# Thresholds of a sparsemax attention: stretched Newton steps, and flagged heads found by rank

## The reference, cut to what matters

```python
x = x + xattn(layernorm(x), ctx)      # q, k, v, o with biases; weights = sparsemax(q k^T / sqrt(32)) over 722 keys
x = x + ffn(layernorm(x))             # sqrt((x cos(theta + n1))^2 + (x sin(phi + n2))^2)

def sparsemax(x):                     # per row: the tau with sum(max(x - tau, 0)) = 1
    zs = -jnp.sort(-x, axis=-1)
    rho = jnp.arange(1, L + 1)
    cssv = jnp.cumsum(zs, axis=-1) - 1.0
    k = jnp.maximum(jnp.sum(zs > cssv / rho, axis=-1, keepdims=True), 1)
    tau = jnp.take_along_axis(cssv, k - 1, axis=-1) / k
    return jnp.clip(x - tau, 0.0)
```

## Time and profile before

| | us |
|---|---|
| median of 3 runs (846.85 to 848.14) | 847.61 |
| the profiled execution, its own time | 848.82 |
| its span | 847.0 |
| DVE busy | 653.7 (77%) |
| PE busy | 600.7 (71%) |
| ACT busy | 373.8 (44%) |
| POOL busy | 205.9 (24%) |
| mean granted clock of PE, share of full speed | 0.84 |

### The profile page before, as it was taken

One profiled execution on the slowest core, in us unless ns is written; L12 is line 12 of the kernel. 1 busy time (PEld: TensorE's weight loads), 2 busy tenths in 40 slices (PEclk: granted clock), 3 DMA queues, 4 the chain that ended last, 5 costly groups with the idle time before them and its releaser, 6 DMA issues.

```text
span 847.0 us, 14807 instructions
## 1 busy us (share of the span) xinstructions
PE 600.7 (71%) x4592; PEld 341.7 (40%) x4592; DVE 653.7 (77%) x3044; ACT 373.8 (44%) x653; POOL 205.9 (24%) x242
## 2 busy tenths in 40 slices
PE   4687228437986099989458998896386498897584
PEld 2344114224543065456233654563143354465251
DVE  5999659659697399999559888996696599999900
ACT  3444216217663056467225565663153265554231
POOL 3643402201403014032301332234004032121101
PEclk9678758858998589999768999999598699997857
DMA  9541110200032000312120212231201101020000
GB/s 324 184 130 44 49 49 3 58 7 25 19 91 57 18 25 17 94 30 70 40 69 0 70 31 56 71 82 28 80 2 55 24 22 48 21 60 11 1 11 10
DMA packets 33458, 44.16 MB, mean 52 GB/s; under 512 B 8347, under 2 KB 26779, under 8 KB 33376
## 3 DMA queue, kind: packets, MB, share of 16 engines
q1 hardware_dynamic: 32320, 41.09, 17.0%
q10 hardware_dynamic: 1056, 2.10, 0.7%
HBM read 23.77 MB, written 1.64 MB: 30 GB/s over the span
## 4 chain that ended last, share of the span: by engine, by line
PE 40%; DVE 30%; issue 18%; ACT 6%; DVEq 2%; DMA 1%; SPq 1%; POOL 1%; POOLq 0%
PE ring L452 19%; DVE cand L913 9%; PE ring L518 6%; PE ring L594 3%; PE mix_bank L567 3%; PE ring L542 3%; PE ring L491 2%; DVE dif L928 2%; DVE f_sum L938 2%; PE ring L503 2%; DVE over L932 2%; ACT S L669 1%; ACT qst L669 1%; DVE dif L933 1%; DVE n_over L940 1%
## 5 line engine op out<-in xcount | busy, mean ns | idle before, releaser
L913 DVE MAX8 cand<-S 100x8 f32<-100x45 f32 (+1 forms) x2048 | 223.1, 189 | 12.3 <-issue 5.2
L452 PE MATMUL ring<-wv,ctx 128*121 128x512 f16 x576 | 161.7, 401 | 0.0
L452 PE MATMUL ring<-ctx,wk 128*128 128x361 f16 x768 | 134.9, 337 | 4.5 <-DVE ctx L1069 4.5
L582 PE MATMUL ring<-ident,tt 100*3 100x100 f16 x128 | 10.7, 244 | 157.3 <-issue 153.0
L785 ACT ACTIVATE pT<-ring 121x800 f32<-121x800 f32 x96 | 80.5, 839 | 85.5 <-PE ring L594 85.5
L669 ACT ACTIVATE S<-ring 100x722 f32<-100x722 f32 x128 | 95.4, 774 | 30.4 <-PE ring L542 29.7
L328 POOL TENSOR_TENSOR ctx<-ctx_f,ctx 128x484 f16<-128x484 f32 x42 | 51.6, 1228 | 211.8 <-ACT ctx L669 211.3
L452 PEld LDWEIGHTS ring<-ctx,wk 128*128 128x128 f16 x768 | 78.4, 104 | 57.7 <-issue 14.1
L669 ACT ACTIVATE qst<-ring 96x800 f16<-96x800 f32 (+1 forms) x32 | 25.7, 829 | 171.8 <-PE ring L582 161.7
L542 PE MATMUL ring<-kst,qst 96*100 96x361 f16 x256 | 68.7, 360 | 29.6 <-ACT S L669 12.5
L452 PEld LDWEIGHTS ring<-wv,ctx 128*121 128x121 f16 x576 | 73.8, 141 | 35.1 <-issue 9.9
(11 more groups left out here) (127 smaller groups left out, 817.2 us busy)
## 6 DMA issues: line engine op xcount, KB each, us to landing
kst<-ks SPq DMA_DIRECT2D x384, 45.1 KB, 1.9
ctx_f<-in_ctx SPq DMA_DIRECT2D x45, 242.0 KB, 2.9
xq<-in_x SPq DMA_DIRECT2D x8, 200.0 KB
xr<-in_x SPq DMA_DIRECT2D x8, 200.0 KB
out_y<-att SPq DMA_DIRECT2D x8, 200.0 KB
S<-in_L_xattn_Wk ACTq DMA_DIRECT2D x1, 1024.0 KB, 6.9
wq<-in_L_xattn_Wq ACTq DMA_DIRECT2D x1, 1024.0 KB, 11.5
wcos<-in_L_ffn_theta SPq DMA_DIRECT2D x1, 1024.0 KB, 10.4
```

The costliest lines, as they stand in the source:

```text
L452: last = nc.tensor.matmul(psum, lhs(c, i), w(c, j), start=(c == 0 and n == 0), stop=(c == DC - 1 and n == 2))
L913: last = nc.vector.max(cand[:, h, 8 * n:8 * n + 8], S[0:L, HH * (i % 2) + h, cuts[n]:cuts[n + 1]])
```

## The change

The stretch factors multiply the first two Newton steps (1.15 and 1.1). The last round looks at seven ranks instead of eight; the first estimate comes from the top value of each piece alone. The eighth rank enters the flag as a count of pieces whose eighth value is below tau, added to the same sum, so `n_edge`, its reduction and its matmul are gone. In `settle`, flagged heads get their number plus one as a code, MAX8 sorts the codes downward, and the sorted list is cast to integers. Its first word says whether there is anything to do; if so, that head is refined directly, then the second word is read, and only if it is not zero a loop of seven turns runs over the rest of the list. `refine` makes one Newton step instead of two ahead of its test, and the test is reduced to one word on DVE (five small maxima) and read with one load instead of four. `NEWTON_MAX` stays 28.

```diff
@@ -26,7 +26,8 @@
 LN_EPS = 1e-5
 SUM_TOL = 1e-5
 PIECES = 16
-RANKS = (2, 4, 6, 8)
+RANKS = (2, 4, 6, 7)
+STRETCH = (1.15, 1.1, 1.0, 1.0)
 NEWTON_MAX = 28
 TINY = 2.0 ** -20
 SCRATCH = 2048
@@ -149,12 +150,13 @@
         dif, over = sb("dif", [L, HH, NCAND]), sb("over", [L, HH, NCAND], BF16)
         fold = sb("fold", [L, HH, 2 + NCAND // 2], BF16)
         tau = sb("tau", [L, 2, HH])
-        f_sum, step_t, n_over, n_now, n_edge = (sb(n, [L, HH]) for n in ("f_sum", "step_t", "n_over", "n_now", "n_edge"))
+        f_sum, step_t, n_over, n_now = (sb(n, [L, HH]) for n in ("f_sum", "step_t", "n_over", "n_now"))
         zero, minus = sb("zero", [L, 1]), sb("minus", [L, 1])
-        flag_i, any_i = sb("flag_i", [1, HH], I32), sb("any_i", [1, 1], I32)
+        order_c, code, ranked = (sb(n, [1, HH]) for n in ("order_c", "code", "ranked"))
+        ranked_i = sb("ranked_i", [1, HH], I32)
         again, againT = sb("again", [P, 32]), sb("againT", [P, 32])
-        again_m = sb("again_m", [P, 1])
-        again_i = sb("again_i", [P, 1], I32)
+        again_m = sb("again_m", [1, P // 32])
+        again_i = sb("again_i", [1, 1], I32)
         count, inv_count, new_sum, delta = (sb(n, [L, 1]) for n in ("count", "inv_count", "new_sum", "delta"))
         eps_t = sb("eps_t", [L, 1])
         st1, mv1, sd1 = sb("st1", [L, 6]), sb("mv1", [L, 2]), sb("sd1", [L, 2])
@@ -526,8 +528,7 @@
                 if i > 0:
                     pe.wait_ge(aT_ready, 2 * i)
                 nc.tensor.matmul(flag_ps, ones[:, :], n_over[:, :], start=True, stop=False)
-                nc.tensor.matmul(flag_ps, minus[:, :], n_now[:, :], start=False, stop=False)
-                nc.tensor.matmul(flag_ps, ones[:, :], n_edge[:, :], start=False, stop=True).then_inc(flag_sum, 1)
+                nc.tensor.matmul(flag_ps, minus[:, :], n_now[:, :], start=False, stop=True).then_inc(flag_sum, 1)
 
             def scores(i, heads):
                 b, part = divmod(i, 2)
@@ -919,9 +920,9 @@
                 t4 = t.rearrange("p (g a c) -> p g a c", a=1, c=1)
                 pieces = cand[:, :, :].rearrange("p g (n r) -> p g n r", r=8)
                 after(found)
-                n = counted(nc.vector.tensor_reduce(f_sum[:, :], pieces[:, :, :, 0:2], AXY, ALU.add))
+                n = counted(nc.vector.tensor_reduce(f_sum[:, :], pieces[:, :, :, 0], AX, ALU.add))
                 after(n)
-                n = counted(nc.vector.tensor_scalar(t, f_sum[:, :], -1.0, 1.0 / (2 * PIECES), ALU.add, ALU.mult))
+                n = counted(nc.vector.tensor_scalar(t, f_sum[:, :], -1.0, 1.0 / PIECES, ALU.add, ALU.mult))
                 for turn, ranks in enumerate(RANKS):
                     E = PIECES * ranks
                     after(n)
@@ -944,23 +945,24 @@
                     n = counted(nc.vector.scalar_tensor_tensor(step_t[:, :], f_sum[:, :], -1.0, step_t[:, :],
                                                                ALU.add, ALU.mult))
                     after(n)
-                    last = nc.vector.tensor_tensor(t, t, step_t[:, :], ALU.add)
+                    last = nc.vector.scalar_tensor_tensor(t, step_t[:, :], STRETCH[turn], t, ALU.mult, ALU.add)
                     if turn < len(RANKS) - 1:
                         n = counted(last)
                 last.then_inc(tau_ready, 1)
                 dve.wait_ge(tau_ready, i + 1)
-                n = counted(nc.vector.tensor_tensor(
-                    over[:, :, :].rearrange("p g (n r) -> p g n r", r=8), pieces,
-                    t4.broadcast_to([L, HH, PIECES, 8]), ALU.is_ge))
+                marks = over[:, :, :].rearrange("p g (n r) -> p g n r", r=8)
+                counted(nc.vector.tensor_tensor(marks[:, :, :, 7:8], pieces[:, :, :, 7:8],
+                                                t4.broadcast_to([L, HH, PIECES, 1]), ALU.is_lt))
+                n = counted(nc.vector.tensor_tensor(marks[:, :, :, 0:7], pieces[:, :, :, 0:7],
+                                                    t4.broadcast_to([L, HH, PIECES, 7]), ALU.is_ge))
                 after(n)
-                n_edge_at = counted(nc.vector.tensor_reduce(
-                    n_edge[:, :], over[:, :, :].rearrange("p g (n r) -> p g n r", r=8)[:, :, :, 7], AX, ALU.add))
                 n = counted(nc.vector.tensor_tensor(fold[:, :, 2:2 + NCAND // 2], over[:, :, 0:NCAND // 2],
                                                     over[:, :, NCAND // 2:NCAND], ALU.add))
                 after(n)
                 n = counted(nc.vector.reduce_sum(n_now[:, :], fold[:, :, :], AX))
                 after(n)
-                nc.vector.tensor_tensor(n_now[:, :], n_now[:, :], n_over[:, :], ALU.min).then_inc(flag_ready, 1)
+                nc.vector.scalar_tensor_tensor(n_now[:, :], n_now[:, :], -float(PIECES), n_over[:, :],
+                                               ALU.add, ALU.min).then_inc(flag_ready, 1)
 
             def newton(p, t, n, total):
                 nc.vector.tensor_scalar(mask_row, p, 0.0, None, ALU.is_gt, ALU.add,
@@ -979,26 +981,28 @@
                 dve.wait_ge(fix, n + 6)
                 return n + 6
 
-            def refine(i, h):
-
-                t = tau[:, i % 2, bass.ds(h, 1)]
-                row = S[0:L, bass.ds(h + HH * (i % 2), 1), :].rearrange("p a n -> p (a n)")
+            def refine(i, number):
+
+                number = nc.s_assert_within(number, 1, HH, skip_runtime_bounds_check_because="inside If(number > 0)")
+                t = tau[:, i % 2, bass.ds(number - 1, 1)]
+                row = S[0:L, bass.ds(number - 1 + HH * (i % 2), 1), :].rearrange("p a n -> p (a n)")
                 dve.sem_clear(fix)
                 nc.vector.scalar_tensor_tensor(relu_row, row, t, zero[:, :].broadcast_to([L, N]),
                                                ALU.subtract, ALU.max, accum_out=new_sum[:, :]).then_inc(fix, 1)
                 dve.wait_ge(fix, 1)
                 n = newton(relu_row, t, 1, new_sum[:, :])
-                n = newton(relu_row, t, n, new_sum[:, :])
                 nc.vector.tensor_scalar(again[0:L, 0:1], new_sum[:, :], 1.0 + SUM_TOL, None, ALU.is_gt).then_inc(fix, 1)
                 dve.wait_ge(fix, n + 1)
                 nc.vector.transpose(againT[:, :], again[:, :]).then_inc(fix, 1)
                 dve.wait_ge(fix, n + 2)
-                nc.vector.reduce_max(again_m[:, :], againT[:, :], AX).then_inc(fix, 1)
-                dve.wait_ge(fix, n + 3)
-                nc.vector.tensor_copy(again_i[:, :], again_m[:, :]).then_inc(fix, 1)
-                dve.wait_ge(fix, n + 4)
-                left = [dve.value_load(again_i[32 * q:32 * q + 1, 0:1], min_val=0, max_val=1) for q in range(P // 32)]
-                with dve.If(left[0] + left[1] + left[2] + left[3] > 0):
+                for q in range(P // 32):
+                    nc.vector.reduce_max(again_m[0:1, q:q + 1], againT[32 * q:32 * q + 1, :], AX).then_inc(fix, 1)
+                n += 2 + P // 32
+                dve.wait_ge(fix, n)
+                nc.vector.reduce_max(again_i[:, :], again_m[:, :], AX).then_inc(fix, 1)
+                dve.wait_ge(fix, n + 1)
+                left = dve.value_load(again_i[0:1, 0:1], min_val=0, max_val=1)
+                with dve.If(left > 0):
                     with dve.Fori(0, NEWTON_MAX) as _:
                         dve.sem_clear(fix)
                         newton(relu_row, t, 0, new_sum[:, :])
@@ -1018,18 +1022,26 @@
                 dve.wait_ge(fix, 5)
 
             def settle(i):
+
                 dve.sem_clear(check_step)
                 dve.wait_ge(flag_sum, i + 1)
-                nc.vector.tensor_copy(flag_i[:, :], flag_ps).then_inc(check_step, 1)
-                nc.vector.reduce_max(any_i[:, :], flag_ps, AX).then_inc(check_step, 1)
+                nc.vector.scalar_tensor_tensor(code[:, :], flag_ps, 0.5, order_c[:, :],
+                                               ALU.is_gt, ALU.mult).then_inc(check_step, 1)
+                dve.wait_ge(check_step, 1)
+                nc.vector.max(ranked[:, :], code[:, :]).then_inc(check_step, 1)
                 dve.wait_ge(check_step, 2)
-                todo = dve.value_load(any_i[0:1, 0:1], min_val=0, max_val=2 * L * NCAND)
-                with dve.If(todo > 0):
+                nc.vector.tensor_copy(ranked_i[:, :], ranked[:, :]).then_inc(check_step, 1)
+                dve.wait_ge(check_step, 3)
+                first = dve.value_load(ranked_i[0:1, 0:1], min_val=0, max_val=HH)
+                with dve.If(first > 0):
                     dve.wait_ge(tau_split, i + 1)
-                    with dve.Fori(0, HH) as h:
-                        rows = dve.value_load(flag_i[0:1, bass.ds(h, 1)], min_val=0, max_val=2 * L * NCAND)
-                        with dve.If(rows > 0):
-                            refine(i, h)
+                    refine(i, first)
+                    second = dve.value_load(ranked_i[0:1, 1:2], min_val=0, max_val=HH)
+                    with dve.If(second > 0):
+                        with dve.Fori(1, HH) as k:
```

(5 more changed lines are left out.)

## The result

The changed kernel takes 821.59 us (four runs, 821.17 to 823.80); the kernel before, on the same chip, 847.23 us. The ratio is 0.9709, 95% interval 0.9679 to 0.9738. The forecast was 816 us, range 802 to 833.

What follows compares the result with a forecast made beforehand. PE and DVE take turns, with PE idle while DVE sits in flagged settles. Terms -92.7 - 12.5 + 78.3 - 5 = -31.9 on 848.8 us give 816.9; the median lies 1.2 lower, so 816 us, range 802 to 833.

Steps and rivals of the forecast that it cites:

- The heads and the loop: Flagged heads fall from seven to three, in settles 3 and 10; head 3 of settle 3 enters the 28-step loop.
- Four settles to the plain path: Four of six flagged settles lose their flags, each falling to 1.13 us: -92.7 us, taken in full.
- The loop: In settle 3, 28 Newton turns of 3.15 us each, 88.2 us, hidden by nothing.
- The rest of the settle: Settle 3 without its 28-step loop: lead-in, two refinements, loads, six idle turns at 1.36 us and the split, 24.6 us.
- Settle 3 as a whole: Settle 3 keeps both flagged heads and gains the 28-step loop: 24.6 + 88.2 - 34.5 = +78.3 us.
- Settle 10: Settle 10 keeps one flagged head, refined without the loop: 9.9 us against 22.4, so -12.5 us.
- Thresholds and ranking: Per half, thresholds save 0.8 us and settle's ranking adds 0.25; over 16 halves between 0 and -9, taken as -5 us.
- The flag stage: In settle, three small operations in a row where two overlapped: +0.25 us a half.
- the last term: The closing -5 us of the sum, for thresholds and ranking over 16 halves.
- the bounds of -7 and -4: Low-side allowances of the range: -7 us for the 28-step loop, -4 us for the thresholds.
- The rival of the refetched loop: Every back jump of the 28 turns waits for its instructions, 28 x 1.9 = 53 us more, 869 us; chance 0.05.

Runs made afterwards that it cites:

- stretch_only: The kernel before with only the stretch factors of the first two Newton steps added; 755.94 us, ratio 0.8925.
- old_thresholds: The changed kernel with the second Newton step put back and thresholds and flags as before, keeping the stretch and new settle; 751.97 us, ratio 0.8882.
- test_first: The changed kernel with the second Newton step put back and the old single flag test in front of the ranking; 740.67 us, ratio 0.8754.
- two_steps: The changed kernel with the second Newton step put back in front of refine's test; 747.98 us, ratio 0.8845.
- loop_4: The changed kernel with NEWTON_MAX 4 instead of 28; 747.13 us, ratio 0.8807.
- second_direct: test_first with the second flagged head also refined directly and the loop over the rest behind a test of the third word; 750.56 us, ratio 0.8857.
- dead_block: test_first with a third copy of refine in the flagged branch that these inputs never reach; 749.7 us, ratio 0.8855.

## Why the prediction was right, and where its terms were not

**The heads and the loop: right.** Three refinements in settles 3 and 10, and one loop of 28 turns, all as counted from the inputs. No view of the profile before could have told this. Without that count the sum would have read about 728 us, since every row of the trace spoke for the change.

**Four settles to the plain path: -92.7 forecast.** Here and below a settle counts from DVE's first instruction on the flags, L1023 before, some 0.07 us ahead of the L1024 of the prediction. The four lengths by the timelines fell from 97.7 us to 2.14 + 1.83 + 1.81 + 1.51 = 7.3, so -90.4. `stretch_only` shows it in the time: -90.5. PE was not late enough to hide any of it that can be measured.

**The loop: 28 x 3.15 = 88.2 forecast, 84.0 measured.** The way round is 0.4 us and not 0.54. The rest of the settle took 26.1 us, 24.6 forecast, although an idle turn of the other loop took 1.17 us and not 1.36. Settle 3 as a whole: +78.3 forecast, 110.1 - 34.5 = +75.6 measured.

**Settle 10: 9.9 us forecast, 11.55 measured** (from L1028 at 591.68 to MAX8 at 603.23). The lead-in was sized by the old one, and the new one has the ranking chain in it, and a cast of 0.68 us. So -10.9 instead of -12.5.

**Thresholds and ranking: -5 forecast, and this step failed.** The experiments put the thresholds at about -4.0 (`old_thresholds`) and the ranking at +7.3 (`test_first`), together +3.3. The sum had -0.8 and +0.25 a half, and its error is in both. Between the kernel before and the changed one, the 16 thresholds together went from 326.8 to 327.0 us. The shortest of them, which meets no collision, fell from 18.78 to 18.39 us: -0.39 and not -0.8. The flag stage is the larger part of that error. Here is half 8 of the kernel before, then half 7 of the changed one, both by the timeline of DVE:

```profile
494.41 1.23 DVE L952 TENSOR_TENSOR over<-cand,tau 100x1024 bf16<-100x1024 f32 x1
495.67 0.38 DVE L956 TENSOR_REDUCE n_edge<-over 100x8 f32<-100x128 bf16 x1
495.97 0.41 DVE L958 TENSOR_TENSOR fold<-over 100x512 bf16<-100x512 bf16 x1
```

```profile
465.43 0.73 DVE L954 TENSOR_TENSOR over<-cand,tau 100x128 bf16<-100x128 f32 x1
465.78 1.30 DVE L956 TENSOR_TENSOR over<-cand,tau 100x896 bf16<-100x896 f32 x1
467.11 0.43 DVE L959 TENSOR_TENSOR fold<-over 100x512 bf16<-100x512 bf16 x1
```

To the start of the fold it was 1.56 us and is 1.68, 0.12 more, where the prediction had 0.15 less. A difference over 896 elements takes 1.09 us, but the comparison of 896, written into every run of eight with one left out, takes 1.30, more than the 1.22 of the full 1024 in a row. The first sum over the top value alone takes 388 ns, before 421 for twice the values, and not 290. It reads 128 values with a stride of eight; that the stride is the reason was not tested. What was left of the saving went into longer holdups: the thresholds lie 32.8 us above 16 times their shortest, before 26.3. These vary from kernel to kernel: `two_steps`, with the same thresholds and the same shortest, takes 323.9 us in all. I did not try to show that they are POOL's; only the cast was tested.

The plain settle grew from 1.34 to 1.97 us, by 0.63 and not by 0.25. The chain of three small operations costs about 0.3 more than the two that overlapped, and the cast's holdups 0.2 on average; the rest lies in register loads and the jump. `test_first` takes 0.57 of it back in some 14 plain settles and gains 7.3 us.

**The sum.** By the timelines the settles and thresholds give -90.4 - 10.9 + 75.6 + 6.3 (the nine settles plain in both) + 0.2 = -19.2 us; the span fell by 25.0. About 5 of the missing 6 us are shorter waits of DVE for PE's flags (9.2 to 5.8 us) and for ACT's standard deviations (7.7 to 5.9 us). The miss of 5.6 us in the total is thus an error of 11 to 12 us in the last term and 4 in the four settles and settle 10, partly made good by the loop and by waits that I had not credited. That these go against each other is luck; the number is closer than its terms. The low end of the range, 802, doesn't follow either: the bounds of -7 and -4 give 805.

**The rival of the refetched loop** (869 us) is out: 27 turns at 3.00 us and `loop_4` leave no room for it. For this loop the rule of the Trainium skill ("Runtime: NRT & Kernel Launch", instruction fetch mechanics) costs nothing that shows: the whole way round takes 0.4 us. This fits a short body that is still held, but no run here changes its length. But the same rule, that a taken branch whose target is outside the window must fetch it first, describes what `second_direct` and `dead_block` met at the long jump forward, where the stops cost 1.9 to 3.3 us more than the usual jump. It doesn't cover the three stops where nothing branches. I had looked for it in the wrong branch.

## What to carry to other kernels

Where a rare branch depends on data, count on the inputs how often it is taken, and how far from its limit each case is, before pricing anything: here one row in 12,800 and one step of 2.6 us decided over 84 us of loop. A fallback loop should run few turns, or test and leave; each idle turn costs its full time where the other engines wait for it, 3.0 us here. Two gains on the same cost overlap, so try each with and without the other. Keep code that is jumped over small, and put the cheapest test in front, since every untaken case pays for it.

## What was not expected of the hardware

A jump over a flagged part with two copies of `refine` takes at most 0.53 us; with three it takes 2.35 to 3.77 us in four of the plain settles and 0.45 to 0.48 in the others, with 57 instead of 49 to 51 packets on the instruction queue. Three stops of 0.7 to 1.4 us come with it where no branch is near. That it isn't each settle fits a target that lies in a page already held in some places and not in others, but which page holds what was not tried.

A DVE cast of eight values out of SBUF, 158 ns alone, took up to 845 ns where it started beside POOL's elementwise work, always to the end of POOL's instruction, and 153 or 154 ns each time with its input in PSUM. The Trainium skill ("GPSIMD Engine Reference", specifications) says that POOL's access to SBUF is shared with DVE and contends with DVE instructions that run in a 2-port mode or have two SBUF inputs. The cast has one SBUF input; the trace agrees if it ran in such a mode, which no run here shows.
